# Feed-forward stage: token blocks of 256 in place of 512, with the next block's rails matmuls and Gelus placed inside the down projection

## The chip, the cores and the metric

One Trainium2 chip, eight cores, one program. Each core works on one of the eight sequences of the batch and holds its own copy of every intermediate in device memory; there is no exchange between cores. The metric is the device time in microseconds of the slowest core. PE is the matmul engine, PEld its weight load, ACT the scalar engine, DVE the vector engine, SP the engine whose queue issues most DMAs; "SPq" and "ACTq" are DMA issues from the queues of SP and ACT.

## The reference

For each sequence of 2048 tokens by 1024 features:

```python
x = x + attention(layernorm(x))            # 16 heads, causal, before the change
# feed-forward, on b = layernorm(x):
y = einsum('btri,hrij->bthrj', xr, rail_maker)      # 4 heads x 64 rails of width 16
z = einsum('bthrj,hrkj->bthrk', y, rail_up_proj)    # 16 -> 64 per rail
h = gelu(z.reshape(b, t, -1))                       # 16384 hidden values per token
x = x + h @ w_cproj.T                               # 16384 -> 1024
```

The kernel folds rail_maker and rail_up_proj into one block-diagonal matrix once (in device memory as w2scr, 32 tiles of 128x512, bf16), so that the rails are one matmul per 128 hidden values and the down projection is a matmul with a contraction of 16384.

## The kernel before, in words

The program first does layer norm, the Q, K and V projections, attention and its output projection. The residual goes to device memory as float32 (xres), and the normalised tokens go there transposed, as bf16 (btscr). Along the way the down-projection weights are cast to bf16 and written to device memory (wcb, 16384x1024). The change touches none of this. It touches the last stage, the feed-forward, lines 930 to 1037.

Before, that stage runs over NBK = 4 blocks of 512 tokens (`for bk`), and each block has three parts, one after the other on PE:

- **The rails.** SP loads the block's transposed tokens (btb, eight DMAs, L950) and then the 32 tiles of w2scr through two buffers (w2b, L960). For each of the 128 groups `mc` of hidden values PE does one matmul of 128x128 weights by 512 tokens (L968) into one of two PSUM banks (pf[6], pf[7]), and ACT writes its Gelu to Hb (L979), which holds 128 x 512 columns in bf16, 128 KB in each partition. A bank is free again when its Gelu is done (`pf_free[zb]`).
- **The down projection.** For each `mc` SP loads 128 rows of wcb (wcs, 256 KB, six buffers, L996), and PE does eight matmuls of 128x128 (a slice of Hb as the weights) by 512 (L1007): four slices of 128 tokens times two halves of the output, accumulating over all 128 `mc` in all eight PSUM banks. Its matmuls wait for `ev_rails`, the block's last Gelu.
- **The output.** DVE adds the residual (xr2, two buffers) to each bank (ob2, L1027), eight adds in a block, and ACT's queue stores ob2 (L1034). The loads of xr2 for the slices 1 and 0 are issued on SP after this (L1019) and wait until the first adds have freed the buffers.

The order of each queue is the order of the program text. A wait is emitted as an instruction ahead of the operation that needs it, on that operation's engine, so whatever stands behind it on that engine or queue stands still too. SP issues all loads of the stage from one queue: xr2, wcs, btb and w2b. The rules that matter: wcs for `mc` waits for the matmuls of `mc - 6`; w2b waits for the last matmul of the tile before the previous one; btb waits for the last rails matmul that read the same buffer; xr2 waits for the add that read it.

Of the kernel before, what the change touches and what calls it, by code (L numbers as in the profile page):

```python
# [129 lines left out]
def build_nc(phase_limit=99):  # L130
# [801 lines left out]
    Hb = p4_es.enter_context(nc.sbuf_tensor("Hb", [128, 128 * SBK], BF16))  # L932
    btb = p4_es.enter_context(nc.sbuf_tensor("btb", [128, 8 * SBK], BF16))
# [11 lines left out]
    btb_free = None  # L945
    hb_free = None

    for bk in range(NBK):
        for oc in range(8):
            P.op("sync", (lambda o_=oc, b_=bk: (lambda e: e.dma_start(  # L950
                out=btb[:, 512 * o_:512 * (o_ + 1)].rearrange("p (a b) -> p a b", a=4),
                in_=btscr_d[4 * b_:4 * (b_ + 1), :, o_, :].rearrange("a p b -> p a b"))))(),
                 waits=ev_btspill + [btb_free] if oc == 0 else (), inc="dtb")
        ev_btb = P.now("dtb")
        zslot = 0
        first_gelu = True
        for h4 in range(4):
            for oc in range(8):
                i = (h4 * 8 + oc) % 2
                P.op("sync", (lambda h_=h4, o_=oc, i_=i: (lambda e: e.dma_start(  # L960
                    out=w2b[i_][:], in_=w2scr_d[h_, o_])))(),
                     waits=[ev_w2s[0], ev_w2s[1], w2b_free[i]], inc=f"dw2{i}")
                ev_wl = P.now(f"dw2{i}")
                for j in range(4):
                    mc = h4 * 32 + oc * 4 + j
                    zb = 6 + (zslot % 2)
                    zslot += 1
                    P.op("tensor", (lambda i_=i, j_=j, o_=oc, z_=zb: (lambda e: e.matmul(  # L968
                        pf[z_][:], w2b[i_][:, 128 * j_:128 * (j_ + 1)],
                        btb[:, 512 * o_:512 * (o_ + 1)], start=True, stop=True)))(),  # L970
                         waits=[ev_wl, ev_btb, pf_free[zb]], inc="t")
                    ev_z = P.now("t")
                    if j == 3:
                        w2b_free[i] = ev_z
                    gw = [ev_z]
                    if first_gelu and hb_free:
                        gw.append(hb_free)
# [37 lines left out]
        for sl4 in (3, 2, 1, 0):  # L1015
# [21 lines left out]
            ob2_free[q4] = P.now(f"dot{q4}")  # L1037

    return finish()


_NC_CACHE = {}

# [44 lines left out]
```

How the kernel before makes its waits and increments, by code:

```python
                def body(eng):  # L115
                    lw = {}
                    for fn, waits, incs in ops_:
                        for (snm, v) in waits:
                            if lw.get(snm, 0) < v:
                                eng.wait_ge(sems[snm], v)
                                lw[snm] = v
                        ins = fn(eng)
                        for (snm, n) in incs:
                            ins = ins.then_inc(sems[snm], n)
# [107 lines left out]
    def finish():  # L232
        for snm in list(P.sems.keys()):
            if snm.startswith("d"):
                tot = P.cnt[snm]
                if tot > 0:
                    P.op("sync", (lambda s_=snm, t_=tot: (lambda e: e.wait_ge(
                        P.sems[s_], t_)))())
        for st in reversed(phase_stacks):
            st.close()
        blk = es.enter_context(nc.Block())
        P.build(blk)
        es.close()
        return nc
```

## Time and profile before

| what | value |
|---|---|
| time, median of 3 runs | 3290.61 us (3289.44 to 3293.22) |
| the profiled execution: time, span of its slowest core | 3290.58 us, 3288.8 us |
| spans of the eight cores | 3278.2 to 3288.8 us |
| PE, ACT, DVE busy over the span | 75%, 29%, 22% |
| the feed-forward stage, from the first load of btb to the end | 1926.9 to 3288.8 us |

How to read it: the profile is of core 0, the slowest. Times are from the start of its span. The busy share of PE is a mean over stages that have different limits, so the stage that the change touches has to be read by itself. Some matmul records are missing in each group (4012 of 4096 stand there for L1007), so a group's count can be below the number in the program.

### The profile page before, as it was taken

The numbers are of one execution on the slowest core, as the hardware profiler recorded it, in microseconds if no ns is written. First come the engines' busy times: TensorE is split into PE (matmuls) and PEld (weight loads), VectorE is DVE, ScalarE is ACT, GpSimd is POOL, SyncE is SP. The second block draws the span as 40 slices with busy tenths as digits, with TensorE's granted clock in tenths as the row PEclk, the third lists the DMA queues.
The fourth block names the chain that finished last, engine by engine and source line by source line (L and its number), as shares of the span: only waits on it lengthen the run. The fifth ranks groups of instructions, "written<-read, shape, count | busy, mean of one in ns | idle before, by whom it ended". The sixth has DMA issues, their size and how long they took to land.

```text
span 3288.8 us, 28684 instructions; the slowest of 8 cores (3278.2 to 3288.8 us)
## 1 busy us (share of the span) xinstructions
PE 2481.9 (75%) x7470; PEld 810.5 (25%) x7582; DVE 720.4 (22%) x1675; ACT 967.4 (29%) x1455; POOL 168.8 (5%) x321
## 2 busy tenths in 40 slices
PE   0258402635988989899699957997799779977998
PEld 0023101201111111111132211442144214431443
DVE  3310475223444444444222210000000000000000
ACT  1322101103555565555211145002700170008000
POOL 0022100022111110000000000000000000000000
PEclk9999755755555555555555555997599859985999
DMA  1122100047666662000222212554255425541554
GB/s 39 58 33 26 13 0 7 7 69 128 137 136 134 136 131 64 0 0 1 39 77 68 76 56 88 154 151 126 79 152 153 138 66 152 153 149 44 163 152 149
DMA packets 188859, 288.17 MB, mean 88 GB/s; under 512 B 40224, under 2 KB 77088, under 8 KB 188704
## 3 DMA queue, kind: packets, MB, share of 16 engines
q1 hardware_dynamic: 134400, 213.96, 21.4%
q0 software_dynamic: 42784, 47.21, 10.8%
q10 hardware_dynamic: 11520, 25.17, 2.0%
q8 instruction: 68, 1.11, 0.1%
q14 instruction: 87, 0.71, 0.1%
HBM read 274.73 MB, written 58.72 MB: 101 GB/s over the span
## 4 chain that ended last, share of the span: by engine, by line
PE 64%; ACT 12%; DVE 10%; issue 7%; DMA 4%; SPq 1%; POOL 1%; DVEq 1%; ACTq 0%; POOLq 0%; another core or an unknown queue 0%
PE pf L1007 27%; PE po L737 8%; PE pat L886 7%; PE ps L661 7%; PE pf L968 5%; ACT Hb L979 4%; PE pc L787 4%; PE pqk L380 4%; PE pqk L494 2%; DMA bbuf<-blkB 2%; ACT ebuf L695 2%; DVE pbuf L715 1%; ACT ddg L643 1%; DMA w2b<-w2scr 1%; SPq L950 1%
## 5 line engine op out<-in xcount | busy, mean ns | idle before, releaser
L1007 PE MATMUL pf<-wcs,Hb 128*128 128x512 bf16 x4012 | 887.1, 381 | 10.5 <-DMA wcs<-wcb 3.0
L979 ACT ACTIVATE Hb<-pf 128x512 bf16<-128x512 f32 x512 | 305.7, 597 | 806.7 <-PE pf L968 780.7
L1007 PEld LDWEIGHTS pf<-wcs,Hb 128*128 128x128 bf16 x4096 | 402.4, 98 | 495.3 <-issue 16.9
L968 PE MATMUL pf<-btb,w2b 128*128 128x512 bf16 x503 | 293.7, 587 | 158.6 <-ACT Hb L979 61.8
L737 PE MATMUL po<-pbuf,Vx 128*65 128x512 bf16 x559 | 350.4, 628 | 79.0 <-DVE pbuf L715 55.0
L661 PE MATMUL ps<-QT,KT 64*128 64x512 bf16 x559 | 336.9, 604 | 0.0
L1027 DVE TENSOR_TENSOR ob<-pf,xr 128x512 f32<-128x512 f32 x32 | 22.1, 692 | 1339.3 <-PE pf L1007 1313.1
L702 ACT ACTIVATE ebuf<-ps,cpool 128x512 bf16<-128x512 f32 x303 | 208.2, 687 | 159.2 <-PE ps L661 125.5
L886 PE MATMUL pat<-owt,Ost 64*128 64x512 bf16 x512 | 224.1, 629 | 23.0 <-DMA owt<-owT 23.0
L695 ACT ACTIVATE ebuf<-ps,cpool 128x1024 bf16<-128x1024 f32 x128 | 142.5, 1113 | 151.9 <-PE ps L661 129.6
L285 PE MATMUL pbt2A<-ident,vts 128*128 128x128 bf16 x64 | 16.5, 257 | 207.0 <-DVE Vx L469 172.7
L715 DVE TENSOR_TENSOR pbuf<-ebuf,dfar 128x512 bf16<-128x512 bf16 x303 | 128.9, 425 | 197.3 <-ACT ebuf L702 171.2
L380 PE MATMUL pqk<-At,wqb 128*128 128x512 bf16 x501 | 132.4, 410 | 38.3 <-ACT QT L389 14.9
L737 PEld LDWEIGHTS po<-pbuf,Vx 128*65 128x65 bf16 x559 | 72.8, 131 | 328.0 <-issue 328.0
L968 PEld LDWEIGHTS pf<-btb,w2b 128*128 128x128 bf16 x512 | 52.6, 103 | 399.2 <-issue 399.0
L715 DVE TENSOR_TENSOR pbuf<-ebuf,ddg 128x512 bf16<-128x512 bf16 x256 | 108.9, 425 | 168.9 <-ACT ebuf L695 151.7
L285 PE MATMUL pbtA<-ident,atm 128*128 128x128 bf16 x64 | 17.0, 265 | 156.2 <-ACT atm L268 91.4
L787 PE MATMUL pc<-rrow,onesF 1*128 1x512 f32 x128 | 132.4, 1135 | 2.5 <-ACT rrow L778 2.5
L661 PEld LDWEIGHTS ps<-QT,KT 64*128 64x128 bf16 x559 | 55.8, 100 | 309.8 <-issue 309.8
L886 PEld LDWEIGHTS pat<-owt,Ost 64*128 64x128 bf16 x512 | 70.2, 142 | 158.7 <-issue 157.0
L251 ACT ACTIVATE lnst<-lnst 128x1 f32<-128x1 f32 x32 | 6.5, 203 | 332.0 <-DVE lnst L248 332.0
L591 POOL DMA_DIRECT2D wcv<-wcT x128 | 67.6, 528 | 429.9 <-DMA wcb<-wcv 423.2
(97 smaller groups left out, 1203.7 us busy)
## 6 DMA issues: line engine op xcount, KB each, us to landing
wcs<-wcb SPq DMA_DIRECT2D x512, 256.0 KB, 2.7
wcv<-wcT POOLq DMA_DIRECT2D x128, 256.0 KB, 4.5
wcb<-wcv SPq DMA_DIRECT2D x128, 256.0 KB, 2.1
w2b<-w2scr SPq DMA_DIRECT2D x128, 128.0 KB, 2.0
xin<-x SPq DMA_DIRECT2D x16, 512.0 KB, 4.0
xrb<-x SPq DMA_DIRECT2D x16, 512.0 KB, 5.0
xres<-xnw ACTq DMA_DIRECT2D x16, 512.0 KB, 5.1
xr<-xres SPq DMA_DIRECT2D x16, 512.0 KB, 5.7
```

The source lines that it names most:

```text
L380: P.op("tensor", (lambda i_=wi, e_=e8, d_=d2, s_=sc: (lambda e: e.matmul(pqk[s_][:], wqb[i_][:, 256 * e_ + 128 * d_:256 * e_ + 128 * (d_ + ...
L591: P.op("gpsimd", (lambda m_=mc, i_=i: (lambda e: e.dma_start(out=wcv[i_][:], in_=wcT_d[128 * m_:128 * (m_ + 1), :])))(), waits=[wcv_st[i]] ...
L661: P.op("tensor", (lambda p_=pr, f_=hf, kc_=kc, hb_=hb, hc_=hc, qc_=qc: (lambda e: e.matmul(ps[p_][:, 512 * f_:512 * (f_ + 1)], KT[hb_:hb_ ...
L695: P.op("scalar", (lambda p_=pr, ci=idxs[0]: (lambda e: e.activation(ebuf[p_][:], ps[p_][:], AF.Exp, bias=cpool[:, ci:ci + 1], scale=1.0))) ...
L702: P.op("scalar", (lambda p_=pr, f_=f, ci_=ci: (lambda e: e.activation(ebuf[p_][:, 512 * f_:512 * (f_ + 1)], ps[p_][:, 512 * f_:512 * (f_ + ...
L715: P.op("vector", (lambda p_=pr, b_=pbi, f_=f, d_=dd: (lambda e: e.tensor_mul(pbuf[b_][:, 512 * f_:512 * (f_ + 1)], ebuf[p_][:, 512 * f_:51 ...
L737: P.op("tensor", (lambda b_=pbi, f2=hf, kc_=kc, h_=h, pb_=pob, f_=first, l_=last: (lambda e: e.matmul(po[pb_][0:65, :], Vx[:, 1040 * kc_ + ...
L787: P.op("tensor", (lambda p_=pob: (lambda e: e.matmul(pc[:], onesF[64:65, 0:128], rrow[64:65, 512 * p_:512 * (p_ + 1)], start=True, stop=Tr ...
L886: P.op("tensor", (lambda h_=h, e_=e2, s_=sl, p_=pi: (lambda e: e.matmul(pat[p_][:], Ost[0:64, S * h_ + 128 * s_:S * h_ + 128 * (s_ + 1)], ...
L968: P.op("tensor", (lambda i_=i, j_=j, o_=oc, z_=zb: (lambda e: e.matmul(pf[z_][:], w2b[i_][:, 128 * j_:128 * (j_ + 1)], btb[:, 512 * o_:512 ...
L979: P.op("scalar", (lambda m_=mc, z_=zb: (lambda e: e.activation(Hb[:, 512 * m_:512 * (m_ + 1)], pf[z_][:], AF.Gelu, bias=0.0, scale=1.0)))( ...
L1007: P.op("tensor", (lambda m_=mc, s_=sl4, e_=e2, p_=pb_i, i_=i: (lambda e: e.matmul(pf[p_][:], Hb[:, 512 * m_ + 128 * s_:512 * m_ + 128 * (s ...
```

## The change

The block becomes SB2 = 256 tokens, so there are NB2 = 8 blocks. Hb and btb are each split into two buffers of half the size (Hb2, btb). The rails of the first block run alone, 128 units. After that the rails of block `bk + 1` are placed inside the down projection of block `bk`: after the matmuls of each `mc`, one unit (one rails matmul of 128x128 by 256 tokens, and one Gelu of 256 columns). The down projection of an `mc` is now four matmuls (two token slices, two output halves), into banks 0 to 3; the rails use banks 4 to 7 in turn. The load of wcs stays one of 256 KB for each `mc` of each block, in six buffers. btb is loaded two blocks ahead, at the top of the loop; the loads of xr2 all stand ahead of the down projection; the output is four adds and two stores in a block.

```diff
--- before.py
+++ after.py
@@ -929,8 +929,12 @@
     P.barrier()
     p4_es = ExitStack()
     phase_stacks.append(p4_es)
-    Hb = p4_es.enter_context(nc.sbuf_tensor("Hb", [128, 128 * SBK], BF16))
-    btb = p4_es.enter_context(nc.sbuf_tensor("btb", [128, 8 * SBK], BF16))
+    SB2 = 256
+    NB2 = S // SB2
+    Hb2 = [p4_es.enter_context(nc.sbuf_tensor(f"Hb2{i}", [128, 128 * SB2], BF16))
+           for i in range(2)]
+    btb = [p4_es.enter_context(nc.sbuf_tensor(f"btb{i}", [128, 8 * SB2], BF16))
+           for i in range(2)]
     w2b = [p4_es.enter_context(nc.sbuf_tensor(f"w2b{i}", [128, 512], BF16)) for i in range(2)]
     wcs = [p4_es.enter_context(nc.sbuf_tensor(f"wcs{i}", [128, D], BF16)) for i in range(6)]
     xr2 = [p4_es.enter_context(nc.sbuf_tensor(f"xr2{i}", [128, D], F32)) for i in range(2)]
@@ -942,55 +946,75 @@
     xr2_free = [None, None]
     ob2_free = [None, None]
     pf_free = [None] * 8
-    btb_free = None
-    hb_free = None
-
-    for bk in range(NBK):
+    btb_free = [None, None]
+    hb2_free = [None, None]
+    rails_done = {}
+    cp_done = {-1: None}
+
+    def load_btb(bk):
+        if bk >= NB2:
+            return
+        p = bk % 2
         for oc in range(8):
-            P.op("sync", (lambda o_=oc, b_=bk: (lambda e: e.dma_start(
-                out=btb[:, 512 * o_:512 * (o_ + 1)].rearrange("p (a b) -> p a b", a=4),
-                in_=btscr_d[4 * b_:4 * (b_ + 1), :, o_, :].rearrange("a p b -> p a b"))))(),
-                 waits=ev_btspill + [btb_free] if oc == 0 else (), inc="dtb")
-        ev_btb = P.now("dtb")
-        zslot = 0
-        first_gelu = True
-        for h4 in range(4):
-            for oc in range(8):
-                i = (h4 * 8 + oc) % 2
-                P.op("sync", (lambda h_=h4, o_=oc, i_=i: (lambda e: e.dma_start(
-                    out=w2b[i_][:], in_=w2scr_d[h_, o_])))(),
-                     waits=[ev_w2s[0], ev_w2s[1], w2b_free[i]], inc=f"dw2{i}")
-                ev_wl = P.now(f"dw2{i}")
-                for j in range(4):
-                    mc = h4 * 32 + oc * 4 + j
-                    zb = 6 + (zslot % 2)
-                    zslot += 1
-                    P.op("tensor", (lambda i_=i, j_=j, o_=oc, z_=zb: (lambda e: e.matmul(
-                        pf[z_][:], w2b[i_][:, 128 * j_:128 * (j_ + 1)],
-                        btb[:, 512 * o_:512 * (o_ + 1)], start=True, stop=True)))(),
-                         waits=[ev_wl, ev_btb, pf_free[zb]], inc="t")
-                    ev_z = P.now("t")
-                    if j == 3:
-                        w2b_free[i] = ev_z
-                    gw = [ev_z]
-                    if first_gelu and hb_free:
-                        gw.append(hb_free)
-                    first_gelu = False
-                    P.op("scalar", (lambda m_=mc, z_=zb: (lambda e: e.activation(
-                        Hb[:, 512 * m_:512 * (m_ + 1)], pf[z_][:], AF.Gelu,
-                        bias=0.0, scale=1.0)))(),
-                         waits=gw, inc="s")
-                    pf_free[zb] = P.now("s")
-        ev_rails = P.now("s")
-        btb_free = P.now("t")
+            P.op("sync", (lambda o_=oc, b_=bk, p_=p: (lambda e: e.dma_start(
+                out=btb[p_][:, SB2 * o_:SB2 * (o_ + 1)].rearrange("p (a b) -> p a b", a=2),
+                in_=btscr_d[2 * b_:2 * (b_ + 1), :, o_, :].rearrange("a p b -> p a b"))))(),
+                 waits=(ev_btspill + [btb_free[p]]) if oc == 0 else (), inc=f"dtb{p}")
+        btb_free[p] = None
+        return P.now(f"dtb{p}")
+
+    btb_evt = {}
+    btb_evt[0] = load_btb(0)
+
+    def rails_unit(bk, u, standalone=False):
+        p = bk % 2
+        h4, rem = divmod(u, 32)
+        oc, j = divmod(rem, 4)
+        i = (u // 4) % 2
+        if j == 0:
+            P.op("sync", (lambda h_=h4, o_=oc, i_=i: (lambda e: e.dma_start(
+                out=w2b[i_][:], in_=w2scr_d[h_, o_])))(),
+                 waits=[ev_w2s[0], ev_w2s[1], w2b_free[i]], inc=f"dw2{i}")
+        ev_wl = P.now(f"dw2{i}")
+        zb = 4 + (u % 4)
+        mwts = [ev_wl, btb_evt[bk], pf_free[zb]]
+        P.op("tensor", (lambda i_=i, j_=j, o_=oc, z_=zb, p_=p: (lambda e: e.matmul(
+            pf[z_][:, 0:SB2], w2b[i_][:, 128 * j_:128 * (j_ + 1)],
+            btb[p_][:, SB2 * o_:SB2 * (o_ + 1)], start=True, stop=True)))(),
+             waits=mwts, inc="t")
+        ev_z = P.now("t")
+        if j == 3:
+            w2b_free[i] = ev_z
+        if u == 127:
+            btb_free[p] = ev_z
+        mc = u
+        gw = [ev_z]
+        if u == 0:
+            gw.append(hb2_free[p])
+        P.op("scalar", (lambda m_=mc, z_=zb, p_=p: (lambda e: e.activation(
+            Hb2[p_][:, SB2 * m_:SB2 * (m_ + 1)], pf[z_][:, 0:SB2], AF.Gelu,
+            bias=0.0, scale=1.0)))(),
+             waits=gw, inc="s")
+        pf_free[zb] = P.now("s")
+        if u == 127:
+            rails_done[bk] = P.now("s")
+
+    btb_evt[1] = load_btb(1)
+    for u in range(128):
+        rails_unit(0, u)
+
+    for bk in range(NB2):
+        p = bk % 2
+        if bk + 2 < NB2:
+            btb_evt[bk + 2] = load_btb(bk + 2)
         xr_evts = {}
-        for sl4p in (3, 2):
-            q4 = sl4p % 2
-            sl = 4 * bk + sl4p
+        for sl2 in (1, 0):
+            q4 = sl2
+            sl = 2 * bk + sl2
             P.op("sync", (lambda s_=sl, q_=q4: (lambda e: e.dma_start(
                 out=xr2[q_][:], in_=xres_d[128 * s_:128 * (s_ + 1), :])))(),
                  waits=[xr2_free[q4], ev_spills[0], ev_spills[1]], inc=f"dr2{q4}")
-            xr_evts[sl4p] = P.now(f"dr2{q4}")
+            xr_evts[sl2] = P.now(f"dr2{q4}")
         for mc in range(128):
             i = mc % 6
             P.op("sync", (lambda m_=mc, i_=i: (lambda e: e.dma_start(
@@ -998,34 +1022,31 @@
                  waits=[wcs_free[i]] + (ev_wcb_done if (bk == 0 and mc < 6) else []),
                  inc=f"dwc{i}")
             ev_wc = P.now(f"dwc{i}")
-            for sl4 in range(4):
+            for sl2 in range(2):
                 for e2 in range(2):
-                    pb_i = sl4 * 2 + e2
-                    mwts = [ev_wc, ev_rails]
+                    pb_i = sl2 * 2 + e2
+                    mwts = [ev_wc, rails_done[bk]]
                     if mc == 0:
                         mwts.append(pf_free[pb_i])
-                    P.op("tensor", (lambda m_=mc, s_=sl4, e_=e2, p_=pb_i, i_=i: (lambda e: e.matmul(
-                        pf[p_][:], Hb[:, 512 * m_ + 128 * s_:512 * m_ + 128 * (s_ + 1)],
+                    P.op("tensor", (lambda m_=mc, s_=sl2, e_=e2, pi=pb_i, i_=i, p_=p: (lambda e: e.matmul(
+                        pf[pi][:], Hb2[p_][:, SB2 * m_ + 128 * s_:SB2 * m_ + 128 * (s_ + 1)],
                         wcs[i_][:, 512 * e_:512 * (e_ + 1)],
                         start=(m_ == 0), stop=(m_ == 127))))(),
                          waits=mwts, inc="t")
             wcs_free[i] = P.now("t")
+            if bk + 1 < NB2:
+                rails_unit(bk + 1, mc)
         ev_cp = P.now("t")
-        hb_free = ev_cp
-        for sl4 in (3, 2, 1, 0):
-            sl = 4 * bk + sl4
-            q4 = sl4 % 2
-            if sl4 <= 1:
-                P.op("sync", (lambda s_=sl, q_=q4: (lambda e: e.dma_start(
-                    out=xr2[q_][:], in_=xres_d[128 * s_:128 * (s_ + 1), :])))(),
-                     waits=[xr2_free[q4]], inc=f"dr2{q4}")
-                ev_xr = P.now(f"dr2{q4}")
-            else:
-                ev_xr = xr_evts[sl4]
+        cp_done[bk] = ev_cp
+        hb2_free[(bk + 2) % 2] = ev_cp
+        for sl2 in (1, 0):
+            sl = 2 * bk + sl2
+            q4 = sl2
+            ev_xr = xr_evts[sl2]
             for e2 in range(2):
-                pb_i = sl4 * 2 + e2
-                P.op("vector", (lambda q_=q4, e_=e2, p_=pb_i: (lambda e: e.tensor_add(
-                    ob2[q_][:, 512 * e_:512 * (e_ + 1)], pf[p_][:],
+                pb_i = sl2 * 2 + e2
+                P.op("vector", (lambda q_=q4, e_=e2, pi=pb_i: (lambda e: e.tensor_add(
+                    ob2[q_][:, 512 * e_:512 * (e_ + 1)], pf[pi][:],
                     xr2[q_][:, 512 * e_:512 * (e_ + 1)])))(),
                      waits=[ev_cp, ev_xr] + ([ob2_free[q4]] if e2 == 0 else []), inc="v")
                 pf_free[pb_i] = P.now("v")
```

## Rows read from the trace of the kernel before

**Rows 1.** Windows of the feed-forward stage on core 0, busy time by engine, granted clock, DMA.
```profile
core 0: us, PE busy (x) PEld busy (x) DVE busy (x) ACT busy (x) POOL busy (x), PEclk, DMA share, GB/s
2036.60:2260.40 223.80, 222.02 (x1003) 100.55 (x1024) 0.02 (x1) 0.00 (x0) 0.00 (x0) 0.99 0.49 145
2260.40:2278.40 18.00, 0.00 (x0) 0.00 (x0) 5.52 (x8) 0.00 (x0) 0.00 (x0) 0.56 0.82 248
2278.40:2375.00 96.60, 73.51 (x126) 13.19 (x128) 0.00 (x0) 76.42 (x128) 0.00 (x0) 0.50 0.20 62
...
3273.70:3288.80 15.10, 0.01 (x1) 0.00 (x0) 5.54 (x8) 0.00 (x0) 0.00 (x0) 0.58 0.57 209
```

**Rows 2.** Chain of waits, core 0: us in total, times, longest us.
```profile
PE pf L968 <- DMA w2b<-w2scr: 59.6, 7, 18.7
```

**Rows 3.** Groups by line with their shapes, core 0: busy us, mean ns.
```profile
L1007 PE MATMUL pf<-wcs,Hb 128*128 128x512 bf16 x4012 | 887.1, 381 | 10.5 <-DMA wcs<-wcb 3.0 <-ACT Hb L979 3.0
L1007 PEld LDWEIGHTS pf<-wcs,Hb 128*128 128x128 bf16 x4096 | 402.4, 98 | 495.3 <-issue 16.9
...
L979 ACT ACTIVATE Hb<-pf 128x512 bf16<-128x512 f32 x512 | 305.7, 597 | 806.7 <-PE pf L968 780.7 <-ACT Hb L979 2.3
...
L702 ACT ACTIVATE ebuf<-ps,cpool 128x512 bf16<-128x512 f32 x303 | 208.2, 687 | 159.2 <-PE ps L661 125.5 <-DVE pbuf L715 11.0 <-DVE Ost L796 10.3
L695 ACT ACTIVATE ebuf<-ps,cpool 128x1024 bf16<-128x1024 f32 x128 | 142.5, 1113 | 151.9 <-PE ps L661 129.6 <-DVE rbt L793 6.5 <-DVE Ost L796 6.3
```

**Rows 4.** Timeline of the stage's start and its rails.
```profile
1926.91 4.39 SPq L950 DMA_DIRECT2D btb<-btscr  x8
...
1936.21 0.63 PE L968 MATMUL pf<-btb,w2b 128*128 128x512 bf16 x1 [12.32 <-issue]
...
1938.18 1.28 ACT L979 ACTIVATE Hb<-pf 128x512 bf16<-128x512 f32 x2
...
1941.14 1.29 ACT L979 ACTIVATE Hb<-pf 128x512 bf16<-128x512 f32 x2 [0.19 <-PE pf L968]
...
1942.62 1.29 ACT L979 ACTIVATE Hb<-pf 128x512 bf16<-128x512 f32 x2 [0.19 <-PE pf L968]
```

**Rows 5.** Timeline from the first rails to the first down projection.
```profile
2027.03 0.90 SPq L990 DMA_DIRECT2D xr<-xres  x2
...
2027.97 16.32 SPq L996 DMA_DIRECT2D wcs<-wcb  x9
...
2036.61 8.58 PE L1007 MATMUL pf<-wcs,Hb 128*128 128x512 bf16 x29 [3.05 <-DMA wcs<-wcb]
...
2040.71 4.20 PEld L1007 LDWEIGHTS pf<-wcs,Hb 128*128 128x128 bf16 x20 [0.16 <-issue]
```

**Rows 6.** The six wcs buffers in mid-projection, 2100 to 2200 us: issues and landing.
```profile
L996 SPq DMA_DIRECT2D wcs<-wcb x58: 319/319/320, 2100.9 to 2199.4; - x58
...
DMA to landing us min/median/max: 2.6/2.8/3.8
```

**Rows 7.** Timeline between the first and the second block.
```profile
2260.38 3.08 DVE L1027 TENSOR_TENSOR ob<-pf,xr 128x512 f32<-128x512 f32 x4 [336.09 <-PE pf L1007]
...
2263.90 9.37 SPq L950 DMA_DIRECT2D btb<-btscr  x8
...
2278.46 1.01 PE L968 MATMUL pf<-btb,w2b 128*128 128x512 bf16 x2 [18.74 <-DMA w2b<-w2scr]
```

**Rows 8.** Windows of 4 us with the DMA engines full, core 0.
```profile
2033.00:2037.00 4.00, 0.95 (x3) 0.20 (x4) 0.00 (x0) 1.19 (x2) 0.00 (x0) 0.50 1.02 384
2266.00:2270.00 4.00, 0.00 (x0) 0.00 (x0) 0.72 (x2) 0.00 (x0) 0.00 (x0) 0.50 1.03 390
2270.00:2274.00 4.00, 0.00 (x0) 0.00 (x0) 2.05 (x3) 0.00 (x0) 0.00 (x0) 0.50 1.05 281
```

**Rows 9.** The same 4 us by core 1's own clock.
```profile
2266.00:2270.00 4.00, 0.00 (x0) 0.00 (x0) 0.45 (x1) 0.00 (x0) 0.00 (x0) 0.50 1.22 296
```

**Rows 10.** Stores of the output over the whole span: issues, KB each, median us to landing.
```profile
out<-ob ACTq DMA_DIRECT2D x16, 512.0 KB, 5.7
```

## The prediction, made before the changed kernel ran

> **What bounds the kernel now.** I read the windows of the feed-forward stage first [rows 1], because the share of busy time on the page mixes stages. A block has three stretches, and in each another thing sets the pace. In the down projection (2036.6 to 2260.4) PE is busy 222.0 of 223.8 us at a granted clock of 0.99, and the DMA engines are half idle (0.49, 145 GB/s): this part is paced by matmuls. In the rails (2278.4 to 2375) ACT is busy 76.4 of 96.6 us, PE holds the lower clock (0.50), and the DMA engines stand at 0.20. Between blocks (18.0 us) no matmul runs and DMA is at 0.82: a stall on transfers. In the waits, seven waits of PE for w2b add up to 59.6 us [rows 2], nearly all of it these gaps. So of a block's period of 338 us (223 + 18 + 97) only 223 are paced by the matmuls of the down projection; the change lays the 97 under them.
>
> **What a unit costs afterwards.** SP issues one wcs per `mc`, 58 between 2100.9 and 2199.4 [rows 6]: 98.5 / 57 = 1.728 us for eight matmuls, so 0.216 us for one of 512 columns at 2.4 GHz, with 98 ns of weight load beside it [rows 3]. A unit of the new loop is four of these plus one of 256 columns, for which I take half, 0.108: 4 x 0.216 + 0.108 = 0.972 us. Seven blocks of 128 such units are 870.9 us; the last block has no rails, 128 x 0.864 = 110.6.
>
> The Gelu of a unit lies beside this. One of 512 columns takes 597 ns [rows 3]. The slope comes from the two Exps: (1113 - 687) / 2 = 213 ns less for 256 columns fewer, so 384 ns. A pair takes 1.29 us [rows 4], 0.09 more than two durations, so 0.474 us for each: under 0.972, hidden. If it were not, PE would wait for banks; with four banks it has about four units (3.9 us) of slack.
>
> **The first rails, alone.** Before, the first rails matmul comes 9.3 us after the first btb issue [rows 4]. Now sixteen smaller btb loads stand ahead of w2b, with the same bytes; the eight took 4.39 us to issue, so between nothing and 4.4 us more: I take 1.3, matmul at 1937.5, first Gelu (2.0 us later, with its table load) at 1939.5. The pairs in the trace repeat every 1.48 us because two banks leave ACT idle 0.19 per pair [rows 4]; with four banks I let ACT run through, 128 x 0.474 = 60.7 us, to 2000.2.
>
> **What is late next: the top of each block.** This is the largest choice. The loop's first act on SP is to load btb two blocks ahead, and this waits for the last rails matmul of the loop before, that is for the end of the projection (call it t0). Queued behind it on SP are both xr2 loads, which wait for the adds, and then every wcs. So none of the six wcs buffers is filled across the boundary, and PE has nothing to do until wcs comes. Step by step: four adds in 3.08 us [rows 7]; eight btb issues in about 4.0 (half of them would be 2.2, at 0.55 each they are 4.4); two xr2, 0.9 [rows 5]; so wcs 0 is issued at about t0 + 4.7. How long it takes behind two xr2 the trace shows: issued at 2027.97, used at 2036.61, 8.6 us [rows 5]. That gives 13.3, and there are now 1.05 MB of stores and 0.52 MB of btb besides. By bytes: 1.05 stores + 1.05 xr2 + 0.52 btb + 1.7 wcs and w2b = 4.3 MB, at 281 to 390 GB/s [rows 8] 11 to 15.3 us. I take 14.5. The two bounds: 6.4 (3.1 for adds, 0.5 to issue, 2.8 to land [rows 6]) if nothing ahead of wcs matters, and the 18.1 of the old boundary [rows 7]. Entering blocks 1 to 5: 5 x 14.5 = 72.5. Entering 6 and 7 there is no btb: wcs 0 issued at about 3.6, plus 8.6: 12.5 each, 25. Entering block 0 there are btb and xr2 but no stores or adds: from the last rails matmul (some 1.4 us before the last Gelu) 4.0 + 0.9 + 8.6, so 12.8 after that Gelu with what btb adds.
>
> After a stall PE starts at 1.2 GHz: from 2036.61 to about 2040.71 weight loads come one by one and the clock is the lower one [rows 5], 4.1 us which at the upper clock would be half: 2 us a block, 16.
>
> **End.** After the last matmul the stage before takes 15.1 us [rows 1] with eight adds. Now four adds (3.1), a store issued behind them, 5.7 to land [rows 10]: 9.
>
> **Sum.** 2000.2 + 12.8 + 870.9 + 110.6 + 16 + 72.5 + 25 + 9 = 3117.0 as span, against 3288.8: 171.8 less. The profiled execution took 1.8 us more than its span and lies at the median of the runs (3290.58 and 3290.61). So 3118.8; I say **3119**.
>
> **Does the stream of weights keep up?** wcb is now read eight times, not four. A unit of 0.972 us needs 262 KB of wcs and a quarter of a w2b tile, 33 KB: 295 KB, 304 GB/s, twice the 145 of now. Share per byte in the projection (0.49 at 145 [rows 1]) would give full engines at 296 GB/s; but with a full queue the same engines moved 384 and 390 GB/s [rows 8], so the share at light load overstates the work. Two cores at once: core 1 had 296 in a window in which core 0 had 390, each by its own clock [rows 8, 9], 686 together against 608 needed. I take "keeps up", narrowly; 281 is the lower bound. The Trainium skill, HBM Reference, Specifications, gives about 358 GB/s for each core when both of a pair stream; by that figure the 304 also fit and the sum stays. No row here shows a long stretch at such a rate.
>
> **Rivals.**
> 1. *The DMA engines pace the units.* At 281 GB/s a unit is 295 / 281 = 1.049 us and one of the last block 0.933: 896 x 0.077 + 128 x 0.069 = +78. At 296 it is +25. Middle about +52: **3171**. For it: linear share, 281 and 296 in full windows. Against it: the 384 and 390. Chance 0.20.
> 2. *The boundaries are short.* If stores and btb don't slow wcs 0, each costs near 6.4: 5 x 8.1 + 2 x 6.1 + 6 = -59: **3060**. For it: wcs 0 lands in 2.8 us on its own. Against it: the 8.6 us with xr2 ahead. A middle way is in my range. Chance 0.14.
> 3. *Latency, not rate; this is the one that ends slower.* A buffer's round is 0.1 + 0.32 to issue, its landing L, and 0.86 of use, and six units must cover it: unit = (L + 1.3) / 6. With L = 2.8 this is 0.68, no bound; from L = 4.5 it binds; at L = 5.5 a unit is 1.14, and 1024 times 0.165 eats the whole gain. At the 5.7 us of the 512 KB stores [rows 10] it is 1.167: 896 x 0.195 + 128 x 0.303 = +213, **3332**. For it: twice the traffic on all cores, landings of 5.7. Against it: those are twice the size, and full windows move more. Chance 0.06. The Trainium skill, HBM Reference, Latency, has 0.2 us for an access on average and 2 us at high load; by that L would be 2.8 + 1.8 = 4.6, a unit 0.983 in all eight blocks, +25 us, 3144. Rows 6 show landings of 2.6 to 3.8 at half load, so nothing here bears the 2 us out yet.
> 4. *The rails matmul does not fit in seamlessly.* Its weight load of 98 ns [rows 3] stands beside only 108 ns of matmul. If one load shows per unit: 896 x 0.098 = +88, **3207**, chance 0.05. If two do, +176, 3295 and so no change, chance 0.03: the change would then not do what it says. Against: at the upper clock 98 ns still fits.
>
> **Numbers.** My forecast holds 0.52. Its own range, boundaries between 11 and 17 us: 3095 to 3140. The range of 8 in 10 takes in rival 2 and all of rival 1: 3060 to 3195. A measurement of this kernel can tell about 0.2% (6.6 us) from no change. Slower by more: rival 3, and 0.01 taken from the forecast for what I have not seen, 0.07; same: rival 4 with two loads, 0.03; faster: the rest, 0.90.
>
> **What would show it.** Right: in the windows between boundaries PE is busy throughout at 0.99 with DMA near 300 GB/s; SP issues a wcs every 0.97 us; eight gaps of PE of 12 to 16 us, put down to wcs. Wrong: PE waits for wcs inside a block with DMA share at 1 (rival 1) or well below 1 and landings over 4.5 us (rival 3); gaps of 6 to 9 us (rival 2); units over 0.97 us with no wait for DMA (rival 4); ACT idle in the first rails, w2b landing late, would stretch the 60.7 us.

## The result, and the profile after

The changed kernel takes 3219.2 us (median of 10 runs) against 3291.8 us for the kernel before in the same session. A few runs fell in a slower state of the chip (3250 and 3308 us of the changed kernel, 3421 of the one before), and the ratio of 0.977, with an interval of 0.974 to 0.979, leaves them out (medians 3214.7 and 3291.6 us). It is faster, by 2.3%. I had forecast 3119, 5.2% faster, with a range up to 3195. The profiled execution took 3192.3 us; its slowest core is core 1, with a span of 3190.8.

The stages ahead of the feed-forward did not move (first load of btb at 1926.8 us, before at 1926.9). In the feed-forward, windows of core 1: the first rails, a gap between blocks, the block behind it, the next pair, the last block, the end.

```profile
1938.00:2011.80 73.80, 41.94 (x128) 13.37 (x128) 0.00 (x0) 50.46 (x129) 0.00 (x0) 0.50 0.29 85
...
2150.30:2164.30 14.00, 0.00 (x0) 0.00 (x1) 2.77 (x4) 0.00 (x0) 0.00 (x0) 0.64 0.78 274
2164.30:2300.50 136.20, 129.72 (x640) 61.54 (x640) 0.00 (x0) 48.86 (x128) 0.00 (x0) 0.99 0.86 269
2300.50:2314.50 14.00, 0.55 (x2) 0.36 (x3) 2.77 (x4) 0.31 (x1) 0.00 (x0) 0.63 0.85 283
2314.50:2450.20 135.70, 129.45 (x640) 60.98 (x637) 0.00 (x0) 48.90 (x128) 0.00 (x0) 0.99 0.87 269
...
3063.00:3184.60 121.60, 113.67 (x507) 47.97 (x505) 0.00 (x0) 0.00 (x0) 0.00 (x0) 0.99 0.85 264
3184.60:3190.80 6.20, 0.00 (x0) 0.00 (x0) 2.77 (x4) 0.00 (x0) 0.00 (x0) 0.80 0.42 169
```

Beside [rows 1]: the block of 223.8 us at 145 GB/s has become two of 136 at 269 GB/s, and the 96.6 us of rails are under them. A gap is 14.0 us; I had said 14.5. But a block's stretch should have been 124.5 + 2 for the cold start, 126.5, and is 136.2. The missing time shows in the waits of PE and in the landing of wcs (the time from the issue of a load until its data are there):

```profile
PE pf L1031 <- DMA wcs<-wcb: 154.2, 123, 14.6
...
L1020 SPq DMA_DIRECT2D wcs<-wcb x1024: 319/320/2193, 2006.1 to 3178.7; - x171
...
DMA to landing us min/median/max: 2.4/4.4/8.0
```

123 waits, of which eight are the gaps; the others lie inside the blocks. Landing has gone from 2.8 us [rows 6] to 4.4. A stretch of the timeline in mid-block shows both kinds of unit:

```profile
2207.51 0.27 PE L981 MATMUL pf<-btb,w2b 128*128 128x256 bf16 x1
...
2208.48 0.27 PE L981 MATMUL pf<-btb,w2b 128*128 128x256 bf16 x1
...
2209.45 0.27 PE L981 MATMUL pf<-btb,w2b 128*128 128x256 bf16 x1
...
2210.43 0.27 PE L981 MATMUL pf<-btb,w2b 128*128 128x256 bf16 x1
...
2210.93 1.02 PE L1031 MATMUL pf<-wcs,Hb 128*128 128x512 bf16 x4 [0.22 <-DMA wcs<-wcb]
...
2211.78 0.27 PE L981 MATMUL pf<-btb,w2b 128*128 128x256 bf16 x1
```

Without a wait a unit takes 0.97 us, the forecast's number. With one it takes 1.35 (2210.43 to 2211.78): the row's 0.22 is only the idle time after the modelled end of the matmul ahead, and the true loss is 0.38. So the sums of such waits in the profile are too small here: 154 us stand there, of which about 110 are gaps, which leaves 44, while the stretches lost (136.2 - 126.5) x 7 + (121.6 - 112.6), 77 us in all.

### The profile page after: what moved, and what is told of

It is laid out like the page before. It is cut to its first block, busy times and chain, and to the rows that moved or that the text cites. A ratio compares the mean times of both kernels' runs of the same rounds, so it can differ in the third digit from the quotient of the medians.

```text
span 3190.8 us, 33580 instructions; the slowest of 8 cores (3173.7 to 3190.8 us)
## 1 busy us (share of the span) xinstructions
PE 2375.4 (74%) x8094; PEld 848.2 (27%) x8094; DVE 720.1 (23%) x1675; ACT 1055.4 (33%) x1967; POOL 168.8 (5%) x321
## 4 chain that ended last, share of the span: by engine, by line
PE 53%; DMA 19%; DVE 10%; ACT 8%; issue 7%; SPq 2%; POOL 1%; DVEq 1%; ACTq 0%; POOLq 0%
DMA wcs<-wcb 16%; PE pf L1031 16%; PE po L737 8%; PE pat L886 7%; PE ps L661 7%; PE pc L787 4%; PE pqk L380 4%; PE pf L981 3%; PE pqk L494 2%; DMA bbuf<-blkB 2%; ACT ebuf L695 2%; DVE pbuf L715 1%; SPq L959 1%; ACT ddg L643 1%; DVE scrW L427 1%
## 5 line engine op out<-in xcount | busy, mean ns | idle before, releaser
L1031 PE MATMUL pf<-wcs,Hb 128*128 128x512 bf16 x4096 | 1009.9, 383 | 155.4 <-DMA wcs<-wcb 154.2
L994 ACT ACTIVATE Hb<-pf 128x256 bf16<-128x256 f32 x1024 | 393.4, 384 | 715.9 <-PE pf L981 693.0
L1031 PEld LDWEIGHTS pf<-wcs,Hb 128*128 128x128 bf16 x4096 | 390.7, 98 | 588.9 <-issue 236.2
L981 PE MATMUL pf<-btb,w2b 128*128 128x256 bf16 x1024 | 287.9, 288 | 36.6 <-issue 14.5
L981 PEld LDWEIGHTS pf<-btb,w2b 128*128 128x128 bf16 x1024 | 101.6, 99 | 179.1 <-issue 75.7
```

Of the source, the lines that this page charges most:

```text
L981: P.op("tensor", (lambda i_=i, j_=j, o_=oc, z_=zb, p_=p: (lambda e: e.matmul(pf[z_][:, 0:SB2], w2b[i_][:, 128 * j_:128 * (j_ + 1)], btb[p_ ...
L994: P.op("scalar", (lambda m_=mc, z_=zb, p_=p: (lambda e: e.activation(Hb2[p_][:, SB2 * m_:SB2 * (m_ + 1)], pf[z_][:, 0:SB2], AF.Gelu, bias= ...
L1031: P.op("tensor", (lambda m_=mc, s_=sl2, e_=e2, pi=pb_i, i_=i, p_=p: (lambda e: e.matmul(pf[pi][:], Hb2[p_][:, SB2 * m_ + 128 * s_:SB2 * m_ ...
```

## The experiments

The changed kernel is the base of each. The time of a run stands with its ratio to the kernel before on the same chip; the changed kernel is at 0.977 (0.974 to 0.979). Where a run was timed once there is no ratio. In the code, "..." and left-out lines stand for what is cut.

**Nine wcs buffers in place of six.**

```diff
-    wcs = [... for i in range(6)]
+    wcs = [... for i in range(9)]
-            i = mc % 6
+            i = mc % 9
```

> Nine wcs buffers in place of six, nothing else. In the changed kernel a block is a gap of 14.0 us and a stretch of 136.2 us, of which 126.5 would be the matmuls; the missing 9.7 us are waits for wcs at 282 GB/s. Theory A (rate): the stream cannot be carried faster than about 282 GB/s, however many loads are in flight. Then a stretch stays within 2 us of 136, the landing time of wcs rises from 4.4 us to about 7, and the time stays within 0.5% of the changed kernel. Theory B (depth): six buffers of one unit each do not cover a landing of 4.4 us and more (rival 3 of the prediction). Then the stretch falls to about 127 us, DMA reaches 300 GB/s in it, and the time falls by about 75 us, to 3120 to 3140.

3213.3 us, 0.970 (0.962 to 0.978): no change that this can tell. Windows on core 1 (2165 to 2290 and 2480 to 2590 us):

```profile
2165.00:2290.00 125.00, 118.71 (x591) 56.69 (x590) 0.00 (x0) 44.93 (x117) 0.00 (x0) 0.99 0.90 276
2480.00:2590.00 110.00, 104.19 (x522) 49.34 (x521) 0.00 (x0) 39.99 (x105) 0.00 (x0) 1.00 0.90 279
```

In mid-block this is the rate of six buffers (282 GB/s from 2180 to 2290 us on core 1 of the changed kernel), and landing rises from 4.4 to 4.9 us on core 1, to 5.3 on the slowest core. I took this for theory A. But two things that I overlooked forbid it. First, inside these blocks nine buffers are hardly in use. The load of w2b stands on SP's queue ahead of every fourth wcs and has only two buffers; before the wcs of unit 4T + 1 it waits for the rails matmul of unit 4T - 5, and that is the unit for which six wcs buffers wait as well. SP's waits on core 1, first from 2165 to 2290 us, where all are for a rails matmul (L981) and none for a wcs buffer, then from 3060 to 3155 us, in the last block, which has no rails and no w2b:

```profile
SPq L120 <- PE pf L981: 57.2, 29, 7.1
...
SPq L120 <- PE pf L1031: 51.0, 108, 0.6
```

Second, in the last block, where the nine are in use, the waits are gone. The last adds of core 1, with six buffers and with nine, and a window of the last block with nine, core 1 and then its neighbour, core 0, each by its own clock:

```profile
3184.67 3.08 DVE L1048 TENSOR_TENSOR ob<-pf,xr 128x512 f32<-128x512 f32 x4 [132.19 <-PE pf L1031]
...
3167.84 3.08 DVE L1048 TENSOR_TENSOR ob<-pf,xr 128x512 f32<-128x512 f32 x4 [120.91 <-PE pf L1031]
...
3065.00:3155.00 90.00, 90.00 (x418) 40.67 (x417) 0.00 (x0) 0.00 (x0) 0.00 (x0) 1.00 0.99 305
...
3065.00:3155.00 90.00, 90.00 (x419) 40.83 (x418) 0.00 (x0) 0.00 (x0) 0.00 (x0) 1.00 1.00 305
```

The last block is 11 us shorter, and on all eight cores it takes 124 to 127 us from adds to adds, against 132 to 135 with six buffers. It asks for 262 KB in 0.864 us, 303 GB/s, as much as a block with rails does. So all cores together can be given this rate, with the DMA share at 1.00, and theory A does not hold there: its loss of 9 us was one of depth (theory B). In the blocks with rails this run does not separate the two. Four w2b buffers beside the nine wcs would have; no run here has them.

**Half of the weight bytes.**

```diff
-                out=wcs[i_][:], in_=wcb_d[128 * m_:128 * (m_ + 1), :])))(),
+                out=wcs[i_][:, 0:512], in_=wcb_d[128 * m_:128 * (m_ + 1), 0:512])))(),
-                        wcs[i_][:, 512 * e_:512 * (e_ + 1)],
+                        wcs[i_][:, 0:512],
```

> Only the first 512 columns of each 128 rows of the down-projection weights are loaded (128 KB instead of 256 KB), and both output halves use them, so half of the weights are left out of the computation; all matmuls stay. Both theories expect the waits for wcs inside a block to vanish: stretches of 126 to 127 us, DMA near 170 GB/s. It measures what the supply of weights costs: 77 us inside the blocks if the prediction's unit of 0.972 us is right, and what it does to the gaps, which by my account (4.3 MB to move, 2.6 now) would fall from 14 to about 11 us. Time about 3085 to 3115. If stretches stay above 130 us, neither theory holds and the unit itself is dearer than 0.972.

3115.2 us, 0.942 (0.935 to 0.949). The window of a block's stretch on core 2:

```profile
2154.00:2281.60 127.60, 126.47 (x627) 63.16 (x638) 0.00 (x0) 48.78 (x128) 0.00 (x0) 0.98 0.58 160
```

PE is busy 126.5 of 127.6 us with every matmul in place. So the units are as cheap as forecast (rival 4 falls). The supply of weights costs 74 us between the two profiled executions (spans of 3190.8 and 3117.2), the 77 of the stretches nearly, and 104 between the medians. The gaps did not fall to the 11 us that I expected: the eight long waits of PE add up to 110 us, 13.8 each. (Half of the wcs bytes is also only 0.8 MB of the 4.3, so 3.5 were left and not 2.6.)

**The loads of btb and xr2 moved behind the first twelve wcs.**

```diff
-        if bk + 2 < NB2: btb_evt[bk + 2] = load_btb(bk + 2)
-        for sl2 in (1, 0): ...        # the xr2 loads
         for mc in range(128):
+            if mc == 12:
+                if bk + 2 < NB2: btb_evt[bk + 2] = load_btb(bk + 2)
+                for sl2 in (1, 0): ...
```

> The loads of btb and xr2 are moved on SP's queue from the top of the block to behind the first twelve wcs loads of the block, so that wcs can be filled across the boundary. My account of the gap (SP's queue held by the wait for the last rails matmul and the adds) expects each gap to fall from 14 us to about 3.5 us, the four adds alone. What this is worth tells A from B again: under A the same 40.4 MB a block must pass at 282 GB/s, 143 us, so a block falls only from 150.2 to about 143 to 145 and the time by 40 to 60 us; under B the block falls to about 140 and the time by 80 to 85.

3214.1 us, 0.971 (0.964 to 0.977): a miss. The gap went as described, and the time did not. Windows on core 1, a gap and the blocks around it:

```profile
2159.00:2305.50 146.50, 130.46 (x638) 60.82 (x636) 0.00 (x0) 48.94 (x128) 0.00 (x0) 0.97 0.91 269
2305.50:2309.00 3.50, 0.00 (x0) 0.00 (x0) 2.77 (x4) 0.22 (x1) 0.00 (x0) 0.80 0.55 80
2309.00:2462.00 153.00, 133.50 (x640) 62.12 (x640) 0.00 (x0) 48.93 (x128) 0.00 (x0) 0.96 0.86 263
```

A block still takes 150 us, all of it now inside the stretch. The windows after show why: in its gaps the changed kernel moved 274 and 283 GB/s. The gap was idle time of PE and not of the stream, and the 40.4 MB of a block take 150 us, 269 GB/s on average, with the gap or without. Why 269 when the last block of the first experiment had 305 stays open.

**wcs filled from a constant tile on the chip** (a source tile `wsrc` in place of `wcb_d`).

> wcs is filled from a constant tile in on-chip memory instead of from device memory, same bytes, same number of issues, same queue; the down projection thus uses constant numbers instead of the weights. If the limit of the stream is device memory (shared by all cores), the waits for wcs inside a block vanish (stretches of about 127 us). If it is the DMA engines themselves, or the depth of six with a similar landing time, they stay at 133 us or more with the DMA share at 0.9.

3124.4 us, timed once. A stretch on core 3:

```profile
2154.00:2280.00 126.00, 124.91 (x637) 62.02 (x635) 0.02 (x1) 48.97 (x128) 0.00 (x0) 1.00 0.80 287
```

The same DMA engines and the same queue carry 287 GB/s at a share of 0.80, with 0.8 us of waits in this stretch, and wcs lands in 2.7 us (median). So what is short is on the side of device memory: its rate, or the time that a load from it takes to land.

**One down-projection matmul of four.**

```diff
                 for e2 in range(2):
+                    if not (mc in (0, 127) or (sl2 == 0 and e2 == 0)):
+                        continue
```

> The changed kernel with only one of the four down-projection matmuls of an mc left (all four at the first and last mc), so three quarters of the down projection are left out; every load, every rails matmul and every Gelu stays. A unit then needs about 0.33 us of PE and 0.47 us of ACT, and only the loads can pace it. Theory A (a limit of device memory near 280 GB/s a core while all cores stream): a block's stretch of 37.7 MB stays at 130 to 140 us, as with all matmuls, and the time stays within 60 us of the changed kernel's 3192. If the 384 and 390 GB/s of the full windows of the kernel before could be held, a stretch would be 98 us and the time about 2900.

3186.5 us, timed once. Windows of two stretches on core 0:

```profile
2161.00:2292.60 131.60, 89.96 (x257) 27.20 (x262) 0.00 (x0) 48.80 (x128) 0.00 (x0) 0.63 0.92 281
2307.00:2436.00 129.00, 91.56 (x255) 26.44 (x258) 0.00 (x0) 48.71 (x128) 0.00 (x0) 0.57 0.95 286
```

Three quarters of the projection are left out, and a stretch falls from 136 to 130 us only. It is not PE that sets the pace. But this run does not tell a rate from a depth either: wcs lands in 5.2 us here (median), and by the sum of rival 3, with 0.63 us of use, a unit is (0.1 + 0.32 + 5.2 + 0.63) / 6 = 1.04 us, while the two stretches have 131.6 / 128 = 1.03 and 129 / 128 = 1.01.

**The changed kernel on four cores**, in two choices of them.

> The changed kernel on cores 0, 1, 4 and 5 alone, so only four of the eight sequences are computed. If the limit is a device memory shared by two neighbouring cores, it stays here: stretches of 134 to 137 us, DMA 265 to 280 GB/s. If it is something that all eight share, this run is already free of it and its stretches are near 127 us.

> The changed kernel on cores 0, 2, 4 and 6 alone, again four of eight sequences. If the limit is a memory shared by two neighbouring cores, each core now has one for itself: no waits for wcs inside a block, stretches of 126 to 127 us, DMA above 295 GB/s in them, landings of wcs near 3 us. If it is the core's own DMA engines, stretches stay at 134 us or more in both four-core runs.

3259.0 and 3257.1 us, each timed once: inconclusive. Both traces name their cores 0 to 3, so they don't tell whether neighbours were apart. No core was free of waits. The cores go in pairs here too: in the second run those named 0 and 1 have spans of 3254 and 3256 us, those named 2 and 3 have 3196 and 3204.

**The changed kernel on one core, and on two.**

> The changed kernel on core 0 alone, so one of the eight sequences is computed. The runs on four cores did not show whether two neighbours shared a memory, since both named their cores 0 to 3; one core alone surely shares nothing. If the limit of the stream near 280 GB/s comes from sharing the device memory, the waits for wcs inside a block vanish: stretches of 126 to 127 us, landings near 3 us, DMA near 300 GB/s. If it is what one core's DMA engines can read from device memory in runs of 2 KB, the stretches stay at 134 us or more at a share of 0.9.

> The same on cores 0 and 1, two of the eight sequences. If neighbours share a memory and this sharing is the limit, one core alone is free of waits and these two show them again, with stretches of 134 to 137 us. If the sharing is wider (four or eight cores), these two are free as well.

3125.4 us on one core, 3207.6 on two, each timed once. Windows, first one core alone, a gap, its stretch and the next stretch:

```profile
2135.90:2149.00 13.10, 1.21 (x3) 0.51 (x4) 2.77 (x4) 0.00 (x0) 0.00 (x0) 0.59 0.90 304
2149.00:2278.00 129.00, 127.24 (x638) 61.41 (x636) 0.00 (x0) 48.72 (x128) 0.00 (x0) 0.99 0.88 283
...
2291.00:2421.00 130.00, 128.40 (x640) 61.77 (x638) 0.00 (x0) 48.73 (x128) 0.00 (x0) 0.98 0.88 282
```

Then core 0 of two:

```profile
2164.00:2305.90 141.90, 131.15 (x640) 61.63 (x640) 0.00 (x0) 48.80 (x128) 0.00 (x0) 0.98 0.84 261
```

One core alone comes within 7 us of my 3119 and is nearly free of waits, though not quite (129 us, not 126.5); wcs lands in 4.0 us there (median), with a neighbour in 4.5. One neighbour more, and the whole loss is back, 82 us, more than the 36 by which the eight-core runs differ among themselves; six more add nothing beyond that. So cores 0 and 1 share something that these loads have to wait for. The eight-core runs bear this out, which I had overlooked: in the timed run of 3221.7 us cores 4 and 5 took 3219.7 and 3220.2 us and the other six 3175 to 3192, and in that of 3226.7 us cores 6 and 7 took 3225.2 and 3221.5 and the others 3178 to 3193, all at the same granted clock (0.73 to 0.74). Neighbours are late together.

**Runs of 4 KB.**

```diff
-    wcb_d = nc.dram_tensor("wcb", [MF, D], BF16, ...)
+    wcb_d = nc.dram_tensor("wcb", [MF // 256, 128, 2, D], BF16, ...)
+            if mc % 2 == 0:
+                    out=wcs[i_][:], in_=wcb_d[m_ // 2].rearrange("p a d -> p (a d)")
```

> The changed kernel with the bf16 weights laid out in device memory so that each partition reads one run of 4 KB for two mc (512 KB a load, four buffers) in place of 2 KB runs; same bytes, same matmuls. The 384 and 390 GB/s on which the prediction leaned were windows with xr2 in them, whose runs are 4 KB. If it is the cost of a run that holds the stream at 280 GB/s, the waits inside a block vanish (stretches near 127 us) and the time falls by about 70 us, to 3125 to 3145. If it is the bytes, through sharing, stretches stay at 134 us or more and the time within 0.5% of the changed kernel.

3200.4 us, 0.971 (0.969 to 0.973): at best 0.6% better, and windows of 136 us of the stage (core 5) still have 281 and 277 GB/s. The size of a run is not the main cause. (The four buffers of this run hold two units each, eight in all.)

**The smaller blocks alone**, with `rails_unit` called for a whole block behind the output of the block before instead of inside `for mc`.

> Half of the change alone: blocks of 256 tokens with the weights read eight times, but the rails of a block stand by themselves ahead of its down projection, as before. A block is then 61 us of rails (ACT, 128 x 0.474), a projection of 33.5 MB that needs 110.6 us of PE and at 282 GB/s 119 us, and gaps; with the rails' stretch the six buffers and the rate are idle again. 8 x (61 + 119 + about 12 to 18) = 1540 to 1580 against 1362 before: time 3460 to 3520. It shows what the smaller block costs by itself, and so what the placing of the rails gives back.

3557.0 us, 1.083 (1.075 to 1.091), dearer than I had expected. The rails with the gap, and the projection, on core 1:

```profile
2142.00:2217.00 75.00, 40.71 (x127) 13.03 (x125) 2.77 (x4) 49.18 (x128) 0.00 (x0) 0.52 0.32 94
2217.00:2341.50 124.50, 117.11 (x516) 49.30 (x516) 0.00 (x0) 0.00 (x0) 0.00 (x0) 0.97 0.88 269
```

So the change is two changes: the smaller block costs 8.3%, and the rails inside the projection give back 10.6 points. The 3460 to 3520 that I expected missed 3557; a projection took 124.5 us and not 119.

**The moved loads again: with nine buffers, with half of the bytes, and on one core.** Each is the edit of the third experiment joined to one above.

> The moved loads of btb and xr2 together with nine wcs buffers. With the moved loads alone the gaps were gone and the blocks still took 150 us at 268 GB/s, though the stream alone (one matmul per mc) passed at 281 to 286. If the difference is that a stream of uneven speed and matmuls of fixed pace wait for each other in turn through only six buffers, nine buffers lift the rate to 280 and a block falls to about 143 to 145 us, the time by 40 to 50 us to 3165 to 3175. If the rate of two neighbours together is simply near 2 x 270, nothing changes (3195 to 3225).

3174.7 us, 0.965 (0.962 to 0.967): the time of the first reading, 1.2 points better than the changed kernel, though neither edit alone did this clearly. But the blocks did not fall to 143 to 145 us; on the eight cores they are 146 to 150 on average (two windows of core 5, 2149 to 2297 and 2297 to 2448 us, still have 269 GB/s), so the hit on the time is in part luck. A good part of the gain is again the last block: 118 to 124 us from adds to adds, against 129 to 136 with the moved loads alone.

> The moved loads with half of the weight bytes (the first 512 columns only, used for both output halves, so half of the weights are left out). Here the stream is far from its limit. My account of the gap says that a gap is then only the four adds, about 3.5 us, so a block is 124.5 + 3.5 to 4 = 128 us in place of 140.9 and the time 3115 - 8 x 12 = about 3015 to 3025. If the gaps come from something other than SP's order, it stays near 3115.

3084.3 us, 0.937 (0.935 to 0.939): 31 us less than 3115, not 95. The boundary is as expected (PE waits 3.1 us for the adds). But the gap came back at mc 12: eight btb and two xr2 in a row hold SP's queue for 5 us, the wcs behind them takes another 6.1 us to land (2145.51 to 2151.61), and six buffers don't last that long. From the timelines of core 7, the queue and PE:

```profile
2140.44 4.00 SPq L959 DMA_DIRECT2D btb<-btscr  x8
2144.53 0.89 SPq L1016 DMA_DIRECT2D xr<-xres  x2
2145.51 0.38 SPq L1021 DMA_DIRECT2D wcs<-wcb  x1
```

```profile
2151.61 1.87 PE L1032 MATMUL pf<-wcs,Hb 128*128 128x512 bf16 x4 [5.68 <-DMA wcs<-wcb]
```

> The moved loads on core 0 alone, one of the eight sequences. One core alone took 3125 with the gaps, at 283 GB/s in the stretches. If what held it there was the queue's order and not the rate, moving the loads now pays: the gaps fall from 13 to 3.5 us, and as the 40.4 MB of a block then need about 135 us at 300 GB/s, a block falls from 142.3 to 132 to 136 us and the time to 3045 to 3080. If 283 GB/s is what one core can read even alone, a block stays at 142 us or more.

3101.9 us, timed once, 24 less than with the gaps: a block is 140.5 us in place of 142.4, neither the 132 to 136 of the first reading nor the 142 or more of the second. Of the 16 us above 124.5 the adds are 3.5, the second gap is 5.5 and the slow clock behind it about 2. A limit of one core does not show: in three windows of 110 us in mid-block PE is busy for 108.7 to 109.4 us, at 291 to 293 GB/s.

**Two passes over the output halves: the stream halved, the rails still inside.** The order of the loops, in outline:

```diff
+    for bk in range(NBK):              # four blocks of 512 tokens again
+        for e2 in range(2):            # banks 0-3, then 4-7
+            for mc in range(128):
+                # wcs: 128 rows x 512 columns, 128 KB, twelve buffers
+                # four matmuls: slices 0..3 of Hb[mc] with this half
+                if bk == 0 and e2 == 0 and mc + 4 < 128:
+                    rails_unit(0, mc + 4, 4)
+                elif e2 == 1 and bk + 1 < NBK:
+                    rails_unit(bk + 1, mc, 0)
```

> Same sums in another order, made to halve the stream: blocks of 512 tokens again (each wcs half tile is used by four matmuls, and wcb is read four times in all), the down projection in two passes, one for each half of the output, in banks 0 to 3 and 4 to 7 in turn. The rails of the next block stand inside the second pass, where Hb of an mc is free after its last use; those of the first block stand inside its first pass, four mc ahead. wcs has twelve buffers of 128 KB, btb two, and btb and xr2 are loaded in mid-pass. Demand is 33.5 + 4.2 MB for 1024 matmuls and 128 rails, about 152 GB/s, half of the changed kernel's. Theory A expects no waits for wcs and no gaps, so the stage is 1939 + 1024 x 0.864 + 512 x 0.216 + about 13 for the end = 2948: time 2940 to 2980. If units are dearer than 0.216 us a matmul (rival 4), it would be above 3000.

2964.0 us, 0.898 (0.896 to 0.900), inside the expected span. Windows on core 0: a pass with rails, a pass without, and again.

```profile
2095.00:2234.80 139.80, 137.31 (x627) 62.41 (x639) 2.77 (x5) 75.96 (x127) 0.00 (x0) 1.00 0.57 165
2234.80:2346.00 111.20, 110.43 (x505) 50.23 (x514) 2.84 (x5) 0.60 (x1) 0.00 (x0) 1.00 0.66 183
2346.00:2485.20 139.20, 137.50 (x628) 62.39 (x639) 2.71 (x5) 75.96 (x127) 0.00 (x0) 1.00 0.56 164
2485.20:2596.30 111.10, 110.33 (x505) 50.16 (x514) 2.75 (x4) 0.60 (x1) 0.00 (x0) 1.00 0.65 184
```

PE hardly stops, at 2.4 GHz (a granted clock of 1.00): 128 x 1.08 = 138.2 and 128 x 0.864 = 110.6 are the matmuls alone. All waits of PE for wcs on this core add up to 5.6 us. It is the fastest version that I ran, 7.9% below the changed kernel.

## Why the prediction was wrong, point by point

- *The unit, 0.972 us*: right. 0.97 wherever nothing waits, and a stretch of 127.6 us with half of the bytes.
- *The Gelu beside it*: right. The mean of one of 256 columns is 384 ns, the forecast's number; it is hidden.
- *The first rails*: the last Gelu ended at 2001.5, forecast 2000.2. Right.
- *The top of the block*: right in size and mechanism, though two of its terms were off and cancelled, which is luck. SP issued wcs 0 at 7.2 us after t0 (2149.8 to 2157.0), not 4.7, since eight btb took 5.95 us and not 4.0; it landed in 7.0 and not 8.6. Gaps of 14.0, forecast 14.5; the first projection began 10.3 us after the last Gelu (2001.5 to 2011.8), forecast 12.8.
- *The end*: 6.2 us, forecast 9. The last store was issued at 3187.8 us and the span ends at 3190.8, so it took 3.0 us and not 5.7.
- *"I take 'keeps up', narrowly"*: **this step failed.** The stretches took 136.2 us for 128 units, (136.2 - 2) / 128 = 1.048 us a unit. The units did wait for wcs, whose landing I had left at the 2.8 us of half the load and which rose to 4.4. In size that is my rival 1 at its lower bound of 281 GB/s (mid-block windows of core 1 have 282 and 281), priced there at +78 us; the stretches lost 77. That the size fits does not make the mechanism right: see rival 3. 3117.0 + 77, less 3 for the end and 1 for the rest, is the profiled span of 3190.8.
- The evidence against rival 1 was misread twice. The 384 and 390 GB/s were windows of 4 us at a boundary, and nothing showed that the neighbour was reading as much at that time. And I added 390 for core 0 and 296 for core 1 from windows that have two different clocks; the sum of 686 was never shown. Over a whole stretch two neighbours had 261 and 269 GB/s in the run on two cores; the most on record is 305 on each of cores 0 and 1 over 90 us, at DMA shares of 1.00 and 0.99 (nine buffers, last block). So 304 was wanted and some 305 could be had with every DMA engine busy and enough loads in flight: there was no reserve.
- *The range*: rival 1 was priced with one rate, and the runs behind the ratio spread from 3192 to 3228 us, while those of the kernel before spread from 3289 to 3294. With half of the bytes and moved loads they are within 3 us. A kernel that waits for something shared varies with it; the profiled execution lay at the low end of that spread, and 27 us of my error of 100 are this.
- *Rival 2* (short gaps): wrong, they were long; and made short by the moved loads they were worth nothing on eight cores. *Rival 3* (latency): not refuted, as I first read it. The landings rose from 2.8 to 4.4 us, and its sum then gives (4.4 + 1.3) / 6 = 0.95 us a unit. (At a landing of 5.5 it gives 1.13, not the 1.14 that I wrote.) That is the last block, 121.6 / 128 = 0.95, and nine buffers took its loss away. For the blocks with rails the sum lacks the wait at w2b, and 1.048 us was measured. *Rival 4*: refuted by half of the bytes.

The Trainium skill, HBM Reference, Specifications, has about 358 GB/s for each core when both of a pair stream, and says that a core alone measures well above its share. The first half was not reached here: with both streaming, each had 261 to 288 in the blocks with rails, and at most 305 in the last block with nine buffers, with the DMA share at 1.00. The second is in its direction (3125 against 3208 us), but no run here could show it: one core alone had 283 GB/s in its stretches, which ask for 304 at the most. By the figures of the same page's Latency, 0.2 us on average and 2 us at high load, an access takes up to 1.8 us more under load (an estimate); the 1.6 that landing rose by is of that size, while with nine buffers it rose by 2.1 to 2.5.

Shown: that the loss is the supply of weights (half of the bytes), that it is on the side of device memory (source on the chip), that one neighbour suffices for it (one core, two cores), and that in the last block it was the depth of six (nine buffers). Not shown: whether in the seven blocks with rails, where 68 of the 77 us were lost, it is a rate of the memory or the small number of loads that the six wcs and two w2b buffers let SP issue ahead. The nine buffers did not reach far there, the run with a quarter of the matmuls fits both, and the 305 GB/s of the last block speak against a fixed ceiling of 281 to 286. Also open: why a block with moved loads still averages 269 GB/s.

## What to carry to other kernels

When a block is made smaller, write down the bytes for each microsecond of the new inner loop before anything else, and compare them with a rate that all cores held for a whole block, not with the fullest window of a few microseconds. Then count how many loads can be in flight, over the whole queue and not for one tile: a load with two buffers in the midst of a stream holds back all that stands behind it, and a run with more buffers tests depth only if SP's waits show that they were used. Laying one stage under another is worth its full length if the bytes don't grow for it: look for an order (here two passes over halves of the output, with Hb refilled behind its last use) that needs no more buffers and no more traffic. And a gap of the bounding engine is worth removing only if the resource behind it is idle in that gap.

## What the runs showed of the hardware that I had not expected

- Two neighbouring cores that read device memory at once had 261 and 269 GB/s over a stretch, one alone 283; DMA share was 0.84 to 0.88 in both cases, so the share does not tell a wait that comes from a neighbour.
- With nine loads allowed in flight and no other load between them, neighbours had 305 GB/s each over 90 us, at a share of 0.99 and 1.00; with six, core 1 had 274 at 0.89 (3080 to 3180 us).
- A load of wcs (256 KB) landed in 2.8 us at 145 GB/s and in 4.4 to 5.3 at 260 to 305; from a tile on the chip in 2.7 at 287.
- A copy of the same shape from a tile on the chip ran at 287 GB/s at a share of 0.80, with 0.8 us of waits in 126.
- Eight issues of btb on SP's queue took 4.0 us in one run and 5.95 in another, and a single issue of wcs up to 2.2 us; in mid-projection of the kernel before, at a DMA share of 0.49, all took 0.32.
